# A Perceiver layer with sparse experts on one core: the next round's rows are turned earlier in each expert round, and round 1's rows come from products

## What is computed

```python
router_logits = x @ gate_w                                # 256 x 64
routing_weights, selected = jax.lax.top_k(router_logits, K)   # K = 8
routing_weights = jax.nn.softmax(routing_weights, axis=-1)
...
gate = jax.lax.ragged_dot(hidden_sorted, gate_proj_w, group_sizes)   # 512 -> 192 per expert
up = jax.lax.ragged_dot(hidden_sorted, up_proj_w, group_sizes)
down = jax.lax.ragged_dot(jax.nn.silu(gate) * up, down_proj_w, group_sizes)  # 192 -> 512
...
out = jnp.sum(out * routing_weights[..., None], axis=1)
```

## Time and profile before

| | |
|---|---|
| Median of 3 runs | 349.67 us (347.76 to 350.11) |
| The profiled execution, its own time | 346.23 us |
| Its span, first to last instruction | 344.5 us |
| Mean granted TensorE clock | 0.978 of full speed |
| Busy over the span: PE, PEld, DVE, ACT, POOL | 308.9, 159.3, 165.5, 101.3, 76.7 us |
| Bytes moved | 91.51 MB, mean 266 GB/s |
| Rounds of experts (28) | from 132.33 us to 339.4 us of the span |

### The profile page before, as it was taken

How to read it: one execution, slowest core, us unless ns; L and a number is a source line. 1 busy time by engine, 2 the same in 40 slices (tenths; PEclk the granted TensorE clock), 3 DMA queues, 4 the chain that set the end, 5 groups by cost and what they waited for, 6 DMA issues and landing times.

```text
span 344.5 us, 8733 instructions
## 1 busy us (share of the span) xinstructions
PE 308.9 (90%) x2653; PEld 159.3 (46%) x2653; DVE 165.5 (48%) x567; ACT 101.3 (29%) x197; POOL 76.7 (22%) x183
## 2 busy tenths in 40 slices
PE   0599999998999967999999999999999999999964
PEld 0463544345775435444444444444544545444431
DVE  7752275774586763344343443434333353434413
ACT  1121301205573333232323223232332323323222
POOL 5000002410000144433322233222332223222310
PEclk9999999998599999899999999999999999999999
DMA  2899997800000004959999749999999999999931
GB/s 66 289 404 399 388 361 250 304 1 1 2 2 2 30 30 118 383 192 367 388 389 397 273 120 362 390 374 332 388 393 332 370 396 386 390 397 384 393 119 63
DMA packets 42363, 91.51 MB, mean 266 GB/s; under 512 B 5144, under 2 KB 13472, under 8 KB 42208
## 3 DMA queue, kind: packets, MB, share of 16 engines
q1 hardware_dynamic: 39600, 83.51, 65.5%
q0 software_dynamic: 2320, 7.60, 6.3%
q10 hardware_dynamic: 416, 0.04, 0.1%
HBM read 90.09 MB, written 1.05 MB: 265 GB/s over the span
## 4 chain that ended last, share of the span: by engine, by line
PE 59%; SPq 15%; DVE 10%; issue 6%; ACT 4%; DMA 3%; POOL 2%; POOLq 1%; ACTq 0%; DVEq 0%
PE psum L1326 14%; PE psum L1370 10%; SPq L402 9%; PE psum L1246 6%; SPq L395 5%; PE psum L1064 4%; PE psum L1076 4%; PE psum L1103 4%; PE psum L1365 4%; DMA store<-n_L_ffn_down_proj_w_dram 3%; PE psum L1164 2%; PE psum L1194 2%; PE psum L1055 2%; DVE store L876 1%; ACT store L959 1%
## 5 line engine op out<-in xcount | busy, mean ns | idle before, releaser
L1326 PE MATMUL psum<-store 128*32 128x384 f32 x896 | 77.4, 486 | 2.7 <-DMA store<-n_L_ffn_down_proj_w_dram 2.6
L1370 PE MATMUL psum<-store 128*32 128x256 f32 (+1 forms) x672 | 60.7, 464 | 6.2 <-DVE store L876 6.1
L890 DVE SCALAR_TENSOR_TENSOR y_parts<-psum,w_slot,y_parts 128x512 fp32r<-128x512 f32 x28 | 21.0, 750 | 61.4 <-ACT y_parts L1026 61.4
L1326 PEld LDWEIGHTS psum<-store 128*32 128x32 f32 x896 | 28.7, 109 | 40.3 <-issue 35.4
L1001 ACT ACTIVATE store<-psum 128x512 f32<-128x512 f32 x29 | 17.3, 597 | 73.0 <-PE psum L1365 72.1
L1246 PE MATMUL psum<-y_parts,place_T 128*128 128x512 f32 x116 | 34.3, 416 | 0.9 <-ACT y_parts L1026 0.9
L566 POOL TENSOR_TENSOR ready<-zero 128x1 f32<-128x1 f32 x29 | 5.7, 195 | 121.8 <-DVE row_no L857 121.3
L567 POOL DMA_INDIRECT store<-x_normed_rows,row_no x29 | 28.2, 972 | 5.3 <-issue 1.8
L871 DVE TENSOR_TENSOR store<-store,psum 128x128 f32<-128x128 f32 x28 | 8.1, 288 | 43.1 <-ACT store L1019 42.6
L1365 PEld LDWEIGHTS psum<-ident,store 128*128 128x128 f32 x112 | 15.7, 210 | 24.7 <-issue 22.6
L1019 ACT ACTIVATE store<-psum 128x192 f32<-128x192 f32 x28 | 9.3, 332 | 54.9 <-PE psum L1326 54.9
(11 more groups left out here) (247 smaller groups left out, 396.1 us busy)
## 6 DMA issues: line engine op xcount, KB each, us to landing
store<-n_L_ffn_gate_proj_w_dram SPq DMA_DIRECT2D x64, 384.0 KB, 7.9
store<-in_L_ffn_up_proj_w_dram SPq DMA_DIRECT2D x64, 384.0 KB, 8.4
store<-n_L_ffn_down_proj_w_dram SPq DMA_DIRECT2D x64, 256.0 KB, 9.8
store<-n_L_ffn_down_proj_w_dram SPq DMA_DIRECT2D x64, 128.0 KB, 9.8
store<-in_L_attn_w_qkv_dram SPq DMA_DIRECT2D x1, 3072.0 KB, 15.1
store<-in_ctx_dram SPq DMA_DIRECT2D x2, 1024.0 KB, 6.7
store<-in_L_attn_w_out_dram SPq DMA_DIRECT2D x1, 1024.0 KB, 17.4
x_sb<-in_x_dram SPq DMA_DIRECT2D x1, 512.0 KB, 4.2
```

Of the source, the lines that this page charges most:

```text
L890: dve.scalar_tensor_tensor(y_parts[:, 1], bank[6], w_slot[:, :], y_parts[:, 0], ALU.mult, ALU.subtract).then_inc(s_yl, 1)
L1326: last = pe.matmul(bank[0][quarter, 0:2 * INTER], xs[:, c, quarter], w[:, :, c, :], start=(c == 0), stop=(c == DC - 1))
L1370: last = pe.matmul(bank[6][quarter, cols], hidT[:, k, quarter], ring[r][:, e, at:at + cols.stop - cols.start], start=(k == 0), stop=(k == 2))
```

## The change

On PE, in each round after the first: `row_numbers` leaves its place behind the gate/up product and stands ahead of the down product; the place and weight products come ahead of `hid`'s transposes; the transposes of the next round's rows come ahead of the whole down product instead of between its two parts. `mix` follows the gate/up product directly. Round 0 makes no mix at all (there is no earlier output, and the two memsets that made it harmless are gone), and gathers round 1's rows by 24 products instead of transposing fetched ones. On POOL no fetch is made for round 1: `fetch(2, 0)` is the first, behind the differences and the split of the weights. On ACT round 0 is written out, without the copy of landed rows. Semaphore counts shift to match.

```diff
@@ POOL
-            pool.memset(place_T[:, :].bitcast(F32), 0.0).then_inc(s_mt, 1)
-            pool.memset(y_parts[:, :, :].bitcast(F32), 0.0).then_inc(s_yl, 1)
...
-            pool.memset(ready[:, :], 0.0).then_inc(s_row, 2)
+            ch.step(pool.memset(ready[:, :], 0.0))
+            pool.memset(ready[:, 0:2], 0.0).then_inc(s_row, 3)
+            pool.memset(ready[:, 2:4], 0.0).then_inc(s_land, 1)
...
-            pool.wait_ge(s_idx, 1)
-            fetch(1, 1)
...
-            pool.reg_mov(pairs, (n + 1) >> 1)
+            pool.reg_mov(pairs, n >> 1)
+            pool.wait_ge(s_xp, 2)
+            pool.wait_ge(s_xd, 32)
+            pool.wait_ge(s_idx, 1)
+            fetch(2, 0)
+            next_round()
+            differences(4)
             with pool.Fori(0, pool.snap(pairs, min_val=1, max_val=TEAMS * TOK // BLK)) as i:
-                for b in range(2):
-                    u = i * 2 + (2 + b)
-                    pool.wait_ge(s_idx, u)
+                for b in (1, 0):
+                    u = i * 2 + (4 - b)
+                    pool.wait_ge(s_idx, u - 1)
@@ DVE
             def write_rows(column, u):
-                dve.wait_ge(s_idp, u)
+                dve.wait_ge(s_idp, u - 1)
...
-            write_rows(1, 1)
@@ ACT
+            def one_round(v, first=False):
+                act.wait_ge(s_gu, v + 1)
+                act.activation(silu, bank[0][:, 0:INTER], ACT.Silu).then_inc(s_si, 1)
+                if not first:
                     act.wait_ge(s_land, v + 1)
                     act.activation(x_rows, landing[:, bass.ds(((v + 1) & 1) * D, D)], ACT.Copy).then_inc(s_row, 1)
@@ PE
             pe.wait_ge(s_flc, 1)
-            pe.wait_ge(s_pk, 2)
-            row_numbers(1)
...
                 if first:
                     pe.wait_ge(s_pk, 3)
-                    pe.wait_ge(s_idx, 1)
                     row_numbers(2)
-                pe.wait_ge(s_pk, v + 4)
-                pe.wait_ge(s_idx, v + 2)
-                row_numbers((v + 3) & (PICKS - 1))
-
-                pe.wait_ge(s_yl, v + 1)
-                pe.wait_ge(s_mt, v + 1)
-                mix(0)
-                mix(1)
-
-                pe.wait_ge(s_h, v + 1)
-                for k in range(2):
-                    last = pe.transpose(bank[1][:, k * P:(k + 1) * P], hid[:, k * P:(k + 1) * P], ident[:, :])
-                last.then_inc(s_htp, 1)
+                    pe.wait_ge(s_xgc, 1)
+                    gather(picks[:, TOK:2 * TOK])
+
+                if not first:
+                    pe.wait_ge(s_yl, v)
+                    pe.wait_ge(s_mt, v)
+                    mix(0)
+                    mix(1)
...
                 last.then_inc(s_mtp, 1)
 
+                pe.wait_ge(s_h, v + 1)
+                for k in range(2):
+                    last = pe.transpose(bank[1][:, k * P:(k + 1) * P], hid[:, k * P:(k + 1) * P], ident[:, :])
+                last.then_inc(s_htp, 1)
+
+                if not first:
+                    pe.wait_ge(s_row, v + 3)
+                    for c in range(DC):
+                        last = pe.transpose(bank[3][:, c * P:(c + 1) * P], x_rows[:, c::DC], ident[:, :])
+                    last.then_inc(s_xg, 1)
+                pe.wait_ge(s_pk, v + 4)
+                pe.wait_ge(s_idx, v + 1)
+                row_numbers((v + 3) & (PICKS - 1))
+
                 pe.wait_ge(s_ht, v + 1)
...
                     if k == 1:
-                        pe.wait_ge(s_row, v + 3)
-                        for c in range(DC):
-                            last = pe.transpose(bank[3][:, c * P:(c + 1) * P], x_rows[:, c::DC], ident[:, :])
-                        last.then_inc(s_xg, 1)
                         pe.wait_ge(s_htt, v + 1)
```

More of the change, by code:

```diff
@@ L552, in _ @@
             pool.memset(rounds[:, TEAMS:], 1).then_inc(s_set, 1)
-            ch.step(pool.memset(zero[:, :], 0.0))
-            pool.memset(ready[:, :], 0.0).then_inc(s_row, 2)
+            ch.step(pool.memset(zero[:, :], 0.0), wait=False)
+            ch.step(pool.memset(ready[:, :], 0.0))
+            pool.memset(ready[:, 0:2], 0.0).then_inc(s_row, 3)
+            pool.memset(ready[:, 2:4], 0.0).then_inc(s_land, 1)
             for h in range(TH):
@@ L568, in fetch @@
                                         bass.IndirectOffsetOnAxis(ap=row_no[:, b:b + 1], axis=0)).then_inc(s_gat[b], 16)
-            pool.wait_ge(s_xp, 2)
-            pool.wait_ge(s_xd, 32)
-            pool.wait_ge(s_idx, 1)
-            fetch(1, 1)
             pool.wait_ge(s_tables, 11)
@@ L625, in _ @@
                     differences(u + 2)
-            pool.wait_ge(s_gat[1], pool.snap(pairs) * 16 + 16)
-            pool.tensor_tensor(ready[:, 2:3], zero[:, :], zero[:, :], ALU.subtract).then_inc(s_land, 1)
+            pool.wait_ge(s_gat[0], pool.snap(pairs) * 16 + 16)
         @block.vector
@@ L1378, in _ @@
                 team_rounds(q, q % RING, q // RING + 1, first=int(q == 0))
-            pe.wait_ge(s_yh, pe.snap(step))
-            pe.wait_ge(s_mt, pe.snap(step) + 1)
+            end = pe.snap(step)
+            pe.wait_ge(s_yh, end)
+            pe.wait_ge(s_mt, end)
             mix(0)
-            pe.wait_ge(s_yl, pe.snap(step) + 1)
+            pe.wait_ge(s_yl, end)
             mix(1, stop=True)
```

26 lines of the change are left out of this document (13 added, 13 removed).

## The result

| | before | after |
|---|---|---|
| Median beside each other, 4 executions each | 349.81 us (347.76 to 350.11) | 339.95 us (338.24 to 340.53) |
| Profiled execution, span | 346.23, 344.5 us | 339.79, 338.1 us |
| Mean granted clock in it | 0.978 | 0.964 |
| Round 2's gate/up starts | 150.33 us | 149.81 us |
| Rounds 2 to 8, each | 7.12 us | 6.52 us |

The ratio of times is 0.972 (95% interval 0.967 to 0.977): faster, by 9.9 us between the medians and 6.4 between the two profiled executions.

A forecast was written before the change was run, and what follows sets the result against it. PE's rounds bound the kernel up to about 260 us, then DMA at its full rate. Terms -4.9 - 1.2 - 0.4 + 2.0 = -4.5 us, from 349.67 to 345.2 us; forecast's own range 341.5 to 347.5, whole range 340.8 to 349.6.

The forecast's parts named there:

- (a): In each round: PE's wait for DVE's copy goes, 0.36 us less.
- (b): In each round: placing products become exposed, 0.25 us more, but cover 0.10 of the wait for `hid`.
- (c): In each round: ACT's copy to `xs` starts early, so the next gate/up's wait for it goes, 0.17 us less.
- (d): In each round: tails follow the down product at once, one change of product kind less, 0.04 us less.
- The start: Before round 2: without round 1's fetch, POOL and fetch 2 come earlier; round 2 starts 2.0 us earlier, at 148.35.
- The release: Round 9's gate/up ends, freeing SP's waiting load and all DMA work behind it, 4.9 us earlier.
- DMA's holes: Behind round 9's release: earlier releases of rounds 13 and 17 fill small gaps in DMA's work, 1.2 us (0 to 1.9).
- Rival (3): Whole kernel: PE alone decides, 13.3 us less, 336.4 us; chance 5%.
- The clock: Last round: PE's longer wait for weights, 5.5 to 7 us, lowers its clock; 2.0 us lost (0 to 4.0).
- (2): Rounds: they hardly shrink, 6.95 us each, as products are pipelined already; time put at 349 us; chance 20%.
- (4): Rounds: fetched rows come late and hold up each round, time about 356 us, slower; chance 5%.
- (1): Last round: the clock stays high, so the 2.0 us loss is absent, 343.2 us; chance 15%.

The follow-up runs named there:

- warm_start: Changed kernel with nine products that compute nothing in PE's idle gaps at 125 to 128 us; 339.11 us, ratio 0.984 to before.
- set 1: Both kernels unchanged, 347.7 and 341.04 us; new round order with before's start, 341.84 us; new start with before's round order, 346.51 us.
- start_only: Changed kernel's start with before's order in all later rounds; 346.51 us, ratio 0.995 to before.
- warm_all: Changed kernel with products that compute nothing at 81.4 to 82.5 us, 125 to 128 us and ahead of the last two weight waits; 333.62 us, ratio 0.962.
- set 3: Changed kernel with products that compute nothing: ahead of the last two weight waits, 339.97 us; in the gaps at 125 to 128 us, 339.11 us.
- set 4: Five products without use at 81.4 to 82.5 us: in before 346.7 us, in the changed kernel 336.31; there with two further filled places 333.62.

## Why the prediction was wrong in size and right in direction

**The round: right in its parts but one, and undersized.** Forecast was 7.12 to 6.70 with a lower end of 6.50; measured is 6.52. The parts are differences of starts, after's from the round shown above and before's from this one:

```profile
231.37 0.20 PE L1288 MATMUL psum<-tok_b,store 128*128 128x1 bf16 x2
231.44 1.17 PE L1246 MATMUL psum<-y_parts,place_T 128*128 128x512 f32 x4
232.44 0.41 PE L1345 MATMUL psum<-ident,store 128*128 128x128 f32 x2
...
233.23 1.06 PE L1370 MATMUL psum<-store 128*32 128x512 f32 x8 [0.23 <-DVE store L876]
234.23 0.75 PE L1365 MATMUL psum<-ident,store 128*128 128x128 f32 x4
234.91 1.07 PE L1370 MATMUL psum<-store 128*32 128x256 f32 x16
235.79 2.76 PE L1326 MATMUL psum<-store 128*32 128x384 f32 x32
```

(a) and (b), DVE's copy and the placing: `hid`, copy and placing took 0.79 of the round (232.44 to 233.23) and take 0.43: -0.36; with the mix and the row numbers, 0.10 more than before, -0.26. Forecast -0.36 + 0.25 - 0.10 = -0.21. (c) and (d), the wait for `xs` and the parts in one: 1.88 to 1.75, -0.13; forecast -0.21. (e) **missing in the sum**: the rows' transposes cost 0.48 where they cost 0.68, -0.20. I had carried the row's 0.68 over to the new place as if it were the price of four transposes; part of it seems to hang on the products beside them. In the run with the rows moved alone they stand directly ahead of the down product and hold PE for 0.66. In after the two row-number products stand between, and 0.48 + 0.12 do for both. Which neighbour takes the price down, `hid`'s transposes ahead or the row numbers behind, no run separates. Over 7 rounds the round's term was 4.2 us in place of 2.9.

**The start: oversized by 1.5 us.** Forecast was -2.0 (bounds 1.5 to 2.6); measured is -0.52 in the profiled pair. It splits in two. Round 0's gate/up starts 0.77 us later than before's (133.10 against 132.33), and from there to round 2 it takes 16.71 us in place of 18.00: -1.29. Fetch 2 was issued at 139.18, not 138.1. I had let POOL's differences come 1.5 us earlier once the fetch ahead of them was gone, but they then wait for ACT's copy of eight products of PE (L1300, through L1007), and started at 133.98, only 0.32 ahead of before's 134.30. Those products and the 24 ahead of them ran at the low clock (1.97 and 2.29 us; before's took 1.10 and 1.52). The slow gate/up itself, 4.36 us, did not hold the fetch up: the row numbers behind it were written at 137.79, and POOL came for them at 138.41. In `warm_start`, without a low clock there, the fetch goes 6.05 us behind round 0's gate/up, where before has 7.24: 1.2 us earlier, so 1.5 was too much even so. The rows were seen 7.06 us after the issue, where the same count gives 6.84 in before; the 6.6 of the forecast is this less 0.2 for POOL. Neither bound took in a stretch of low clock ahead of round 2 in a new place, though before has one from 138 to 142 us. Undisturbed, the start is worth 0.6 to 1.8 us (set 1).

**The release.** Forecast -4.9, measured 203.15 - 198.40 = 4.75: two errors of +1.3 and -1.5 that cancel.

**DMA's holes: undersized.** From the release to the last round's start it took 331.19 - 203.15 = 128.0 us, and takes 323.66 - 198.40 = 125.3: -2.8; forecast -1.2, bound 1.9. It is no accident of one pair: this stretch takes 124.9 to 125.5 us in all nine profiles of the new round with whole loads, and 128.0 to 128.8 in four of the old. Before's holes stand behind the waits for rounds 13 and 17: it moves 289 and 333 GB/s in the two windows from 232 to 240 us, 325 and 336 in those from 260 to 268, and against 390 that is an estimated 2.8 us of work. After moves 380 to 398 in the like windows of its own (222 to 238 and 246 to 262 us), and has no hole. I took a third of the 3.7 that the rows gave, for starting and ending which the trace doesn't show. The halved loads confirm that DMA bounds: 15.35 us of gain where nothing waits for it. Rival (3), PE alone, had forecast 13.3 (its 26 rounds hold the last one already, so the 0.4 for that is counted twice), and would have been near if the bytes were lighter.

**The clock: right.** The forecast had 2.0 us lost in the last round, with 5 to 7 us of waiting ahead of it. Measured: gate/up +1.7 (4.48 for 2.79), 13.31 to 14.44 in all, +1.13 with the shorter round taken off it; the forecast's two terms, +2.0 and -0.4, made +1.6. The 5.7 us of waiting stand ahead of the round before the last; the last itself waits 2.32 us. In before 2.61 us of waiting had left the clock high; 2.32 us do not here. That the round ahead had run low itself is not the reason needed: in start_only 2.68 us of waiting behind rounds at the full clock gave a gate/up of 4.24 us. What tips it at such lengths stays open. The Trainium skill, "TensorE: Matmul & The Clock Gate", section "Why this matters for your kernels", says that idle gaps between bursts throw the clock to its low level; the runs agree in the main: 4.48 us without work in the gaps, 2.79 with it, though before's gap of 2.61 us did not do it.

**The base: the step that missed by most.** The profiled pair sums to -4.75 - 2.8 + 1.13 = -6.4, 1.9 us more than the forecast's -4.5. The rest is the 3.4 between before's profiled execution and its median, which I added to 341.7 as if it were constant. Most of it goes with the clock: over the 57 executions of before in the five sets, the time falls as the mean granted clock rises, 344.5 to 344.9 us at 0.988, 345.6 to 347.3 at 0.978, 347.5 to 349.9 at 0.973, 349.6 to 350.4 at 0.969 (not strictly: one at 0.964 took 349.62). The profiled one had 0.978 and was a quick one; the clocks of those that make up the median are not on record. Not all is the clock: the store of the output took 1.2 us more in one of two profiles of before. After's, at 0.964, was an ordinary one of its kernel, 339.79 beside a median of 339.95, so there is nothing to add. Without the offset the forecast would have been 341.7, 1.9 off. Either miss alone would have left the time inside the range: with the terms right and the offset added it is 343.3. This also explains most of the three sizes for one change. At like clocks the kernels differ by more than the pair does: 348.0 and 338.24 at 0.975, 350.0 and 340.3 at 0.970, 344.8 at 0.988 and 336.17 at 0.985, so 8.6 to 9.8. Worked out without the clock, an estimate, the change is -0.6 to -1.3 for the start (`warm_all`, `warm_start`), -4.2 for the rounds, -2.8 for DMA's holes and -0.6 for the last round: -8.2 to -8.9. After gives part of that back, as it runs more at the low clock.

**Rivals.** (2) is out: no round is 6.95. (4) is out from round 2 on: L1364 waits once, 1.2 us, in round 1; in no other round. (1) is out in after, though it can be made: set 3 and set 4. Two of the signs of being wrong that the prediction named came: a DMA rate off by more than 1%, and a fetch 2 seen later than 7 us after its issue.

## What to carry to other kernels

Price a moved group by what stands on both sides of it in its new place, not by its row in the old one: the same four transposes held PE for 0.68, 0.66 and 0.48 us. When PE is made faster in front of a DMA that is at its rate, ask what it does while it waits, since the clock takes some of the gain back; products without use in those gaps and in earlier ones were worth 6.3 us here between the medians of two sets (339.95 and 333.62), beside the change's own 9.9. A time that moves by 2% from execution to execution wants the granted clock beside each number before an offset is added to a forecast. And an operation that loses the work ahead of it starts earlier only up to its next wait: POOL's differences gained 0.32 us, not 1.5.

## What the runs showed of the hardware

- **The clock falls in the same code in some executions and not in others.** The stretch at 84 to 92 us has 0.50 to 0.57 in twelve of the thirteen profiles without the five products and 1.00 in the other, start_only's, though the code up to there is the same; 5 products in a gap of 1.1 us ahead of it gave 1.00 in all four profiles that had them. What makes it fall without them stays open.
- **Time at the low clock costs some 0.4 of its length here,** an estimate from the executions of before. Between 0.988 and 0.969 lie 0.019 x 2 x 346 = 13 us more at the low level, and 5.3 us of time (344.8 to 350.1).
- **One stretch removed can put another in its place.** Before with the five products lost the clock from 124 to 128 and 134 to 138 us instead. With all three places filled the four executions took 332.99 to 334.38, where before has 343.27 to 351.26; but the same places with SP's hold gave 332.57 to 335.45 and a low stretch at 142 to 146 us, and four executions say little of a spread (the new order alone had 341.39 to 342.32).
- **Waits of nearly one length left the clock high in one profile and low in another:** 2.61 and 2.49 us in two of before, with a gate/up of 2.79 behind them, and 2.68 in start_only's, with 4.24.
- **The store of the output, 2 x 256 KB, landed 2.2 us after its issue in fifteen profiles,** and 3.2 and 3.4 in two of before's code, at the very end of the span.
- **A row fetch of 256 KB beside a backlog of loads** took 6.1 to 7.8 us from issue to being seen, whether it was issued at 134 or 139 us, and holding back a third of the team's load took off at most 1 us (6.1 and 6.9, beside 7.1 and 7.8).
